# A decoder layer in split fp32: rows at the head of SyncE's units, waits per bank, and a new order at the start of the token-number steps

## The reference

```python
x = x + attn(layernorm(x))            # 16 heads of 128, tanh softcap 50, causal, sigmoid gate per head
x = x + by_token_number(layernorm(x)) # expert = token id // 6250 (4 of them); Wg = Wu = Wd = ctx[e]
x = x + moe(layernorm(x))             # shared expert (704) + top 2 of 8 experts (352 each)
```

```python
g = silu(x @ ctx[e].T); u = x @ ctx[e].T; y = (g * u) @ ctx[e].T   # 512 x 512
```

## Time and profile before

| | |
|---|---|
| median of 3 runs | 1598.95 us (1597.19 to 1600.09) |
| the profiled execution's own time | 1597.67 us |
| its span | 1595.9 us |
| mean granted TensorE clock | 0.995 of full speed |
| PE busy | 1560.7 us, 98% of the span |
| DVE, ACT, POOL busy | 65%, 37%, 28% |

### The profile page before, as it was taken

One profiled execution on the slowest core, in us unless ns is written; L12 is line 12 of the kernel. 1 busy time (PEld: TensorE's weight loads), 2 busy tenths in 40 slices (PEclk: granted clock), 3 DMA queues, 4 the chain that ended last, 5 costly groups with the idle time before them and its releaser, 6 DMA issues.

```text
span 1595.9 us, 24237 instructions
## 1 busy us (share of the span) xinstructions
PE 1560.7 (98%) x7964; PEld 1351.2 (85%) x7965; DVE 1042.2 (65%) x2231; ACT 583.7 (37%) x997; POOL 447.5 (28%) x378
## 2 busy tenths in 40 slices
PE   7999999999999999999999999999999999999996
PEld 6888788888888888888888887788999989999995
DVE  4898777788887788887787778646663572222221
ACT  4454443434444334344334343333111322333331
POOL 4445332134123234222233221103200003333342
PEclk9999999999999999999999999999999999999998
DMA  8786663676886786886686875565631036768753
GB/s 296 283 298 231 205 231 128 240 290 248 295 300 224 261 303 243 292 308 223 245 309 249 300 306 224 175 210 159 228 101 45 8 124 207 224 188 279 199 91 46
DMA packets 106241, 351.65 MB, mean 220 GB/s; under 512 B 11104, under 2 KB 32096, under 8 KB 100640
## 3 DMA queue, kind: packets, MB, share of 16 engines
q1 hardware_dynamic: 93120, 312.63, 54.7%
q0 software_dynamic: 13024, 37.79, 10.0%
HBM read 227.18 MB, written 123.19 MB: 220 GB/s over the span
## 4 chain that ended last, share of the span: by engine, by line
PE 78%; DMA 12%; DVE 5%; issue 2%; POOL 1%; ACT 1%; SPq 0%; POOLq 0%; DVEq 0%; ACTq 0%
PE bank L362 25%; PE bank L364 25%; PE bank L363 25%; DMA out<-x_early,ids_e 11%; PE bank L1936 1%; DVE resid L1264 0%; DVE stats L1094 0%; DMA rows<-x_rows,ids_e 0%; POOL wqk L653 0%; POOL store L653 0%; PE bank L2053 0%; PE bank L2010 0%; DVE place_hot L1618 0%; DVE tile_vals L1628 0%; DVE resid L1457 0%
## 5 line engine op out<-in xcount | busy, mean ns | idle before, releaser
L694 POOL TENSOR_TENSOR probs<-probs,causal 128x256 f32<-128x256 f32 x126 | 90.3, 737 | 411.5 <-ACT probs L872 411.5
L364 PE MATMUL bank<-store,wqk 128*128 128x512 f32 x512 | 202.4, 395 | 0.0
L363 PE MATMUL bank<-store,wqk 128*128 128x512 f32 x512 | 202.1, 395 | 0.0
L362 PE MATMUL bank<-store,wqk 128*128 128x512 f32 x512 | 201.9, 394 | 0.0
L1264 DVE SCALAR_TENSOR_TENSOR resid<-bank,factor,resid 128x512 f32<-128x512 f32 x256 | 189.2, 741 | 1.5 <-PE bank L364 1.4
L653 POOL TENSOR_TENSOR pre_split<-pre_raw,pre_split 128x1528 fp32r<-128x1528 f32 x34 | 120.3, 3539 | 141.0 <-ACT pre_split L834 141.0
L870 ACT ACTIVATE probs<-bank 128x512 f32<-128x512 f32 x189 | 85.9, 529 | 131.4 <-PE bank L364 131.4
L364 PEld LDWEIGHTS bank<-store,wqk 128*128 128x128 f32 x512 | 96.2, 188 | 22.7
L363 PEld LDWEIGHTS bank<-store,wqk 128*128 128x128 f32 x512 | 96.2, 188 | 20.7
L362 PEld LDWEIGHTS bank<-store,wqk 128*128 128x128 f32 x512 | 96.3, 188 | 19.6
L1295 DVE TRANSPOSE_TENSOR_REDUCE bank<-probs 128x16 f32<-128x512 f32 (+3 forms) x256 | 108.4, 492 | 0.0
(11 more groups left out here) (333 smaller groups left out, 4033.5 us busy)
## 6 DMA issues: line engine op xcount, KB each, us to landing
pre_parts<-pre_split SPq DMA_DIRECT2D x34, 1528.0 KB, 6.5
wqk<-wqk_parts SPq DMA_DIRECT2D x96, 512.0 KB, 5.0
pre_raw<-pre SPq DMA_DIRECT2D x34, 764.0 KB, 7.8
store<-wv_parts SPq DMA_DIRECT2D x12, 2048.0 KB, 9.3
wo<-wo_parts SPq DMA_DIRECT2D x48, 512.0 KB, 8.4
expert_w<-pre_parts SPq DMA_DIRECT2D x8, 2816.0 KB, 11.5
wqk_parts<-wqk SPq DMA_DIRECT2D x16, 1024.0 KB, 5.0
expert_w<-pre_parts SPq DMA_DIRECT2D x8, 1536.0 KB, 9.0
```

The lines of the kernel that those rows point to most:

```text
L362: nc.tensor.matmul(out_ap, a_hi, b_hi, start=first, stop=False)
L363: nc.tensor.matmul(out_ap, a_hi, b_lo, start=False, stop=False)
L364: return nc.tensor.matmul(out_ap, a_lo, b_hi, start=False, stop=last)
L694: nc.gpsimd.tensor_tensor(diagonal, diagonal, causal[:, :, :], ALU.mult).then_inc(S["masked"], 1)
```

## The change

In SP's loop the stores and loads of normalised rows go from the tail to the head of the iteration. For the last outputs PE waits, per bank, for the addition that frees that bank, in place of all four. Row tile 2 of the token-number steps is loaded plain and transposed by PE between the up and down products of step 1; DVE no longer turns it. DVE's statistics of the last batch are done two after step 1 and two after step 2, and the rows are applied after step 3. PE's steps 2 to 17 are written out instead of looped. POOL's pieces of shared weights wait two steps longer.

```diff
--- before.py
+++ after.py
@@ -481,6 +481,16 @@
             fills = [(xs, "zero_filled_x", at) for at in range(0, XTILES, ZTILES)]
             sp.wait_ge(S["zeros_ready"], 1)
             for u in range(U):
+                b, h = divmod(u, HEADS)
+                if b + 1 < BATCH and LN_IN + 3 <= h < LN_IN + 6:
+                    half = TB // 2
+                    first = TB * (b + 1) + half * (h - LN_IN - 4)
+                    if h > LN_IN + 3:
+                        for t in range(first, first + half):
+                            turn_xn(t)
+                    if h < LN_IN + 5:
+                        for t in range(first + half, first + 2 * half):
+                            store_xn(t)
                 if u > HEADS:
                     if u - 1 == HEADS:
                         sp.wait_ge(S["wo_stored"], 16 * HEADS)
@@ -519,16 +529,6 @@
                     store_wqk(u + 1)
                     if u + 2 < HEADS:
                         sp.dma_start(wqk_raw[:, :, :, :], wqk_in[u + 2]).then_inc(S["wqk_loaded"], 16)
-                b, h = divmod(u, HEADS)
-                if b + 1 < BATCH and LN_IN + 3 <= h < LN_IN + 6:
-                    half = TB // 2
-                    first = TB * (b + 1) + half * (h - LN_IN - 4)
-                    if h > LN_IN + 3:
-                        for t in range(first, first + half):
-                            turn_xn(t)
-                    if h < LN_IN + 5:
-                        for t in range(first + half, first + 2 * half):
-                            store_xn(t)
                 if 2 <= u < 2 + len(fills):
                     rows_of, done, at = fills[u - 2]
                     fill(rows_of, done, at, min(ZTILES, rows_of.shape[0] // P - at))
@@ -550,6 +550,9 @@
             def load_row(ph, source, g, j):
                 load_turned(rows[:, j, :], source[bass.ds(g * P, P)], S[f"{ph}_row{j}"])
 
+            def load_plain(ph, source, g, j):
+                sp.dma_start(rows[:, j, :], source[g * P:(g + 1) * P]).then_inc(S[f"{ph}_row{j}"], 16)
+
             def store_y(ph, target, g, j):
                 sp.wait_ge(S[f"{ph}_y_out"], g + 1)
                 sp.dma_start(target[bass.ds(g * P, P)], rows[:, 2 + j, :]).then_inc(S[f"{ph}_y_stored{j}"], 16)
@@ -559,7 +562,7 @@
                 g = 2 * i + j
                 if load:
                     sp.wait_ge(S[f"{ph}_xT_ready"], g + 1)
-                    load_row(ph, source, g + 2, j)
+                    (load_plain if first else load_row)(ph, source, g + 2, j)
                 if not first:
                     store_y(ph, target, g - 1, 1 - j)
 
@@ -572,8 +575,8 @@
 
             for i in range(TB):
                 sp.wait_ge(scat[i], 16 * (BATCH - 1))
-            for j in range(2):
-                sp.dma_start(rows[:, j, :], xs[j * P:(j + 1) * P]).then_inc(S[f"x_row{j}"], 16)
+            load_plain("x", xs, 0, 0)
+            load_plain("x", xs, 1, 1)
             sp.wait_ge(S["k_ready"], U)
             load_ct(2)
             load_wo(U - 1)
@@ -741,7 +744,7 @@
                 (sh_down_hi, 0, CT_COLS + SH_UP_COLS, SC // 2), (sh_down_lo, 1, CT_COLS + SH_UP_COLS, SC // 2)) for k in range(0, to.shape[1], n)]
             pool.wait_ge(S["pre_stored"], 16 * PRE_JOBS)
             for n, (to, part, first) in enumerate(pieces):
-                pool.wait_ge(S["x_xT_ready"], n + 5)
+                pool.wait_ge(S["x_xT_ready"], n + 7)
                 flat = plain(to.rearrange("p k n -> p (k n)"))
                 nc.gpsimd.dma_start(flat, pre_parts[:, part, first:first + flat.shape[1]]).then_inc(S["sh_loaded"], 16)
 
@@ -1419,11 +1422,10 @@
 
             p_last()
 
-            def ln_stats_x():
+            def ln_stats_x(first, end):
                 dve.wait_ge(S["y_added"], TB * U)
-                for i in range(TB):
+                for i in range(first, end):
                     ln_stats(ln, TB * (BATCH - 1) + i)
-                ln_eps(ln)
 
             def ln_apply_x():
                 for i in range(TB):
@@ -1443,7 +1445,7 @@
 
             def turn_rows_x(i, j):
                 dve.wait_ge(S["x_xT_lo"], 2 * i + j)
-                dve.wait_ge(S[f"x_row{j}"], 16 * QUADS * i + 16)
+                dve.wait_ge(S[f"x_row{j}"], 16 * QUADS * i + (16 if j else 32 - 16 * QUADS))
                 turn(rows[:, j, :]).then_inc(S["x_xT_ready"], 1)
 
             def turn_x3(t):
@@ -1520,17 +1522,19 @@
             step("x", 0, first=True, between=fourth_y)
             for i in range(TB - 1):
                 y_add(U - 1, i, TAIL_BANKS[1][i])
-            turn_rows_x(1, 0)
-            step("x", 1, between=ln_stats_x)
+            step("x", 1)
             turn_rows_x(1, 1)
-            ln_apply_x()
+            ln_stats_x(0, TB // 2)
 
             def step_and_turn(i, j):
                 step("x", 2 * i + j)
                 turn_rows_x(i + 1, j)
 
             step_and_turn(1, 0)
+            ln_stats_x(TB // 2, TB)
+            ln_eps(ln)
             step_and_turn(1, 1)
+            ln_apply_x()
             by_twos(dve, step_and_turn, 4, XTILES - 2)
 
             def take_x(*tiles):
@@ -1895,9 +1899,9 @@
                 output(U - 2, i, TAIL_BANKS[0][i])
 
             def transpose_rows_x(g):
-                pe.wait_ge(S[f"x_row{g}"], 16)
+                pe.wait_ge(S[f"x_row{g % 2}"], 16 * (g // 2) + 16)
                 for k in range(KC):
-                    last = nc.tensor.transpose(bank[XT][:, k * P:k * P + P], every(rows[:, g, :], k), ident[:, :])
+                    last = nc.tensor.transpose(bank[XT][:, k * P:k * P + P], every(rows[:, g % 2, :], k), ident[:, :])
                 last.then_inc(S["x_xT_ready"], 1)
 
             def up(ph, g, products, first, between=None, to=0):
@@ -1956,9 +1960,11 @@
                 e = pe.value_load(expert_x[0:1, bass.ds(g, 1)], min_val=0, max_val=TOKEN_EXPERTS - 1)
                 return [lambda k, w=P, m=m: m[0:w, bass.ds(e, 1), k, :].rearrange("p a n -> p (a n)") for m in (ct_hi, ct_lo)]
 
-            def x_step(i, j, last=False, second=True):
+            def x_step(i, j, last=False, second=True, rows_next=0):
                 g = 2 * i + j
                 up("x", g, [matrix(g)], False)
+                if rows_next:
+                    transpose_rows_x(rows_next)
                 if not second:
                     pe.wait_ge(S["y_added"], TB * (U - 1) + 1)
                 down("x", g - 1, *matrix(g - 1), second, (lambda: transpose_act_last("x")) if last else None)
@@ -1973,13 +1979,15 @@
             up("x", 0, [matrix(0)], True, to=X_FIRST)
             transpose_rows_x(1)
             for i in range(TB):
-                pe.wait_ge(S["y_added"], TB * (U - 1) if i < TB - 1 else TB * (U - 2))
+                if i < TB - 1:
+                    pe.wait_ge(S["y_added"], TB * (U - 2) + TAIL_BANKS[1][i] + 1)
                 if i == TB - 1:
                     pe.wait_ge(S["x_act"], 1)
                 output(U - 1, i, TAIL_BANKS[1][i])
             transpose_act("x", 0)
-            x_step(0, 1, second=False)
-            by_twos(pe, x_step, 2, XTILES - 1)
+            x_step(0, 1, second=False, rows_next=2)
+            for g in range(2, XTILES - 1):
+                x_step(g // 2, g % 2)
             x_step((XTILES - 1) // 2, (XTILES - 1) % 2, last=True)
             transpose_x3(0)
             down("x", XTILES - 1, *matrix(XTILES - 1), False, to=X_LAST, parts=last_parts("x"))
```

## The result

The changed kernel takes 1589.36 us in the median of 4 runs (1587.76 to 1591.29), the one before 1599.52 us beside it: ratio 0.9937, 95% interval 0.9919 to 0.9955, so 7 to 13 us faster. The direction and the places were right, the size was too small: two terms that I had put at nothing were worth 0.9 and 0.8 us.

A forecast was written before the change was run, and what follows sets the result against it. PE, busy 98% of the span, was taken to bound the kernel, so only its pauses could give time. 4.0 us (unit 10) + 2.9 (start of the steps) = 6.9, from 1598.95 to 1592.0 us; range 1589.5 to 1596.5.

The forecast's parts named there:

- SyncE's move in batch 0: Unit 10: fetching rows earlier removes the pause and the low clock behind it, gain 4.04 us.
- SyncE's move in batches 1 and 2: Attention in batches 1 and 2: nothing to be gained, since PE has no pause there.
- The weights of units 26 and 42: Fetched tiles ahead of unit 26's q half cost 1.5 us; it still lands 1.5 us early, no cost taken.
- the slower rival: Units 26 and 42: two fetched tiles hold the queue 8.2 us, weights come late, 1605.9 us; chance 0.04.
- The start of the steps: First token-number steps: of 4.23 us lost, VectorE's new order and PE's transposes win 2.9, bounds 1.5 and 3.8.
- The remainders of 0.25 and 0.6 us: Losses expected to remain on PE after steps 1 and 3, using 1.18 us for the sequencer.
- straight code: I take 0: PE's steps 2 to 17 written out: gain 0, since steady steps already hold 5.97 us.
- the straight code gives more: If 0.73 us of issue at 1010.25 is a branch's fetch, step 3's remainder vanishes: 1591.4; chance 0.03.
- Step 4: Token-number step 4 carries the four normalisations, 1.98 us on VectorE, and comes out level.
- Waits per bank: Unit 63's outputs: the first goes earlier, the stall moves by three products; gain 0, bounds 0 and 1.3 us.
- PE's transposes for VectorE's turn, and the statistics: Steps' start: PE pays 0.47 us, VectorE loses 1.10 us of work; aT_lo no longer stands behind the statistics.
- Pieces two steps later: GpSimd's shared weights: 0.9 us of idle left, first gather should not move; bounds 0 and a us.

The follow-up runs named there:

- run 5: The changed kernel unchanged, timed again: 1590.18 us against 1598.51 for the kernel before, ratio 0.9945.
- run 9: The changed kernel with PE's steps 2 to 17 as a loop of pairs again: 1591.67 us, ratio 0.9955 to the kernel before.
- run 8: The changed kernel with all four statistics in step 1 and rows applied after tile 3's turn, as before: 1591.16 us, ratio 0.9954.
- run 10: The changed kernel with the last outputs waiting for all four additions of unit 62 again: 1589.28 us, ratio 0.9950.
- run 7: The changed kernel with row tile 2 loaded and turned by VectorE as before: 1589.98 us, ratio 0.9947.
- run 11: The changed kernel with GpSimd's pieces of shared weights at the steps of before: 1593.27 us, ratio 0.9974.
- run 3: The kernel before without the 39 indirect additions of routed experts: 1591.46 us against 1596.74 with them, ratio 0.9957.
- run 4: The changed kernel without the 39 indirect additions of routed experts: 1583.13 us, ratio 0.9906 to the kernel before.
- run 6: The changed kernel with SyncE's move in batch 0 only, at the tail in batches 1 and 2: 1590.73 us, ratio 0.9950.
- run 2: The changed kernel with SyncE's stores and loads of rows back at the tail: 1593.48 us, ratio 0.9978 to the kernel before.
- run 12: The changed kernel with VectorE's key sums of unit 63 behind step 0's activation product: 1588.13 us, ratio 0.9942.

## Why the prediction was right or wrong

**SyncE's move in batch 0: right.** 4.0 us forecast; unit 10 went from 18.95 to 14.91 us, pause and clock, and is 14.91 to 14.92 in all eleven profiles that have the move there.

**SyncE's move in batches 1 and 2: the step that failed first.** I wrote that nothing is to be gained there, "since PE has no pause there". The 1.21 us for which VectorE waited in unit 26 were in the trace, in a row that I had not weighed; I took one execution's lack of a PE pause for the rule. The wait there only just fitted into VectorE's 1.2 us of room. The tail order loses 0.9 us there in the mean of four profiles, where my sum had 0.

**The weights of units 26 and 42: nearly right.** No execution lost there what the slower rival asked for (its pause is 416.16 to 421.4, 5.2 us and not 5.3, which changes nothing). But the slack was smaller than I had worked out. SyncE's issue of the two halves for unit 42 before, then in the profile after SyncE in unit 41 and PE at unit 42's q product:

```profile
645.23 3.81 SPq L438 DMA_DIRECT2D wqk<-wqk_parts  x2
```

```profile
637.54 7.26 SPq L375 DMA_DIRECT2D rows<-xn_rows  x8
644.84 1.62 SPq L475 DMA_DIRECT2D xn_rows<-rows  x2
646.50 0.46 SPq L442 DMA_DIRECT2D wo<-wo_parts  x1
647.01 1.19 SPq L438 DMA_DIRECT2D wqk<-wqk_parts  x2
```

```profile
654.37 0.28 PE L364 MATMUL bank<-q_hi,k_lo 128*128 128x256 f32 x1
654.71 0.50 PE L362 MATMUL bank<-store,wqk 128*128 128x512 f32 x1
```

SyncE took 7.26 us to issue eight row loads, so the q half went out at 647.0, 7.7 us before PE began with it. Before, it went out at 645.2, 11.9 us ahead (PE began at 657.16). So it was issued 4.2 us later, not "at most a us later than now", and PE paused about 0.2 us. Two of the ten profiles show unit 41 longer, by 0.3 us. The cost came from the issue, not from the bytes ahead of it: before, the half landed 8.6 us after its issue, and in run 5, whose unit 41 is the other long one, 7.6.

**The start of the steps: mechanism right, the sum too small.** I forecast 2.9 us out of bounds of 1.5 and 3.8; 3.6 were measured. The remainders of 0.25 and 0.6 us that I left standing after steps 1 and 3 are there when PE has its loop (transposes to up 0.63 and 1.09 us against 0.39) and not in straight code (0.39 and 0.48). So the term that failed is "straight code: I take 0". I judged it by the steady steps, where the sequencer has its lead anyway; I used 1.18 us for the sequencer where straight code needs less. Rival "the straight code gives more" was right in its outcome, 0.84 us by run 9, but not in its condition. The 0.73 us of "issue" at 1010.25 was no branch: in the records of PE's sequencer there is none ahead of that up product, only the load of the expert number, which took 0.57 us there, and run 8 shows the like in straight code (0.54 us). The loop's cost stands ahead of up 2 and up 4. The section "Instruction fetch mechanics" of the Trainium skill ("Runtime: NRT & Kernel Launch"), by which a taken branch out of the fetched window waits for a fetch, pointed the same way; the trace does not show a fetch, only the sequencer's branch and register operations in a place where nothing covers them. Step 4 was not quite level: it takes 6.09 to 6.15 us in straight code (4 to 18 is 83.67 us against 83.52), so by up 18 the start has gained 3.5 us, and straight code 0.7 of it.

**Waits per bank: right, 0** (run 10). The first output came 1.3 us earlier after the last q_hi copy, as forecast; that it stands at 987.02 and not 4.0 below 989.4 is because this execution was already 1.7 us behind at the q_hi copy of unit 2. **PE's transposes for VectorE's turn, and the statistics: right in sign**; 0.9 and 2.3 us by the profiles of runs 7 and 8. With the 0.84 of run 9 that is 4.0, more than the 3.6 of all three together, so they are not independent.

**Pieces two steps later: the gather right, the purpose missed.** The gather did not move, with 1.3 us left where I had 0.9. But the later pieces are not free of effect: with the new order the scattered rows land later (the first piece waited for them until 1016.9 before and 1021.9 after), and without the shift three pieces would meet a row tile's load (run 11). Even so two meet it, and the first profile lost 1.5 us at step 7; other executions lost nothing or 0.2 to 0.6 us.

**Sum.** 4.0 + 0.9 + 3.6 = 8.5 us, less a few tenths for step 4, late row tiles and weights. Runs 3 and 4 have 8.3, run 5 has 8.8. My 6.9 lacks the 0.9 and the 0.8. The first comparison's 10.2 us has 8.5 inside its interval of 7 to 13; a single median of 4 runs at 1589.36 lies below 1590.4 (1598.95 less 8.5) by what single runs of this kernel scatter. So that the time came out below my range is in part chance; that the sum was 1.6 us short is not. Where executions scatter, the fourteen profiles show: the stretch to the q_hi copy of unit 2 takes 52.6 to 54.6 us, unit 13 takes 15.3 to 16.5, and the end behind PE's last product 13.8 to 16.3. What remains open is how often units 26 and 42 pause before: four profiles are few, and the times of run 6 do not settle it.

## What to carry to other kernels

A wait that costs nothing in one trace can cost in the next: where an engine waits for a DMA and the pause just fails to reach the bound engine, count it as a term with a chance, not as 0. Two or three profiles give the room (1.2 us in unit 26, 1.7 us in the steps); a wait costs what exceeds it. Judge straight code against a loop not by steady passes but by the passes in which the bound engine's sequencer has just been held: there the loop's count and branch stand in the open. And when a change moves one burst of DMA later, look at which load it now meets.

## What the runs showed of the hardware

Bulk loads of 708 KB on GpSimd's queue and a row tile's four 64 KB loads on SyncE's queue met at step 7. With two pieces 3.2 to 4.1 us apart VectorE waited 3.16 us for the tile in the first profile, 0.92 to 1.96 us in six others (runs 2, 5, 6, 7, 10 and 12) and not at all in runs 4 and 9; with three at once it was 4.42 us (run 11), and the time of eleven runs went up with it. That the pieces are the cause is shown by run 11 alone; why the same two cost so differently is open.

Eight row loads of 64 KB took SyncE between 3.65 and 7.26 us to issue in the same profile. The slow eight went out right behind a store of 1.5 MB, and one issue of them took 2.66 us. The DMA engines were as busy beside the fast eight (share 1.03 against 0.96), so that does not explain it; the cause is open. That the issue itself slows down, and not only the landing, I had not expected.

On PE a loop's branch took 0.22 to 0.24 us when it was taken and 0.08 when it was not (run 9); in the steady steps none of it shows, they take 5.97 us with the loop and without.

Leaving out 39 additions that PE never waits for made the kernel before 5.3 us faster (1591.46 against 1596.74), though two of its units were longer. All of it lies behind PE's last product: from there to the end the profiles have 15.6 us with them and 8.4 without.
